# Gated linear attention and a gated FFN on one core: K and Q of rows 1 to 3 spread by DMA, outer products in the scan's layout, gate and state in PSUM

## The reference

```
q, k, v = x@Wq, x@Wk, x@Wv                      # 16 heads x 8
gate = exp(log_sigmoid(x@Wgk1@Wgk2 + b) / 16)   # per head and v channel
for t: S[h,v,k] = S[h,v,k]*gate[t,h,v] + v[t,h,v]*k[t,h,k]
       o[t,h,v] = sum_k S[h,v,k]*q[t,h,k]
x = layernorm(x + (layernorm(o)*gamma + beta) * silu(x@Wg) @ Wout)
```

```
h = silu(x@w1*s1) * (x@w2*s2)                   # 128 -> 512
h = gelu(h@h1*s3);  h = gelu(h@h2*s4)           # 512 -> 512, twice
x = layernorm(x + h@w3*s5)                      # 512 -> 128
```

## Time and profile before

| | us |
|---|---|
| median of three runs | 193.88 |
| the profiled execution | 193.71 |
| its span, first to last instruction | 191.9 |
| TensorE busy (matmuls) | 162.0 |
| VectorE busy | 147.9 |
| ScalarE busy | 117.5 |
| GpSimd busy | 113.8 |
| mean granted TensorE clock, share of full speed | 0.982 |
| DMA: 8.65 MB, mean 45 GB/s, nearly all ahead of 25 us | |

### The profile page before, as it was taken

One profiled execution on the slowest core, in us unless ns is written; L12 is line 12 of the kernel. 1 busy time (PEld: TensorE's weight loads), 2 busy tenths in 40 slices (PEclk: granted clock), 3 DMA queues, 4 the chain that ended last, 5 costly groups with the idle time before them and its releaser, 6 DMA issues.

```text
span 191.9 us, 2751 instructions
## 1 busy us (share of the span) xinstructions
PE 162.0 (84%) x790; PEld 124.0 (65%) x790; DVE 147.9 (77%) x301; ACT 117.5 (61%) x188; POOL 113.8 (59%) x94
## 2 busy tenths in 40 slices
PE   1859988969499997999999699999987999799840
PEld 1638656849387774878768487677856866567630
DVE  1398886988788997998999997899999685512360
ACT  4633649898037725378682556768454688979623
POOL 8989589919706689580677688427782313470011
PEclk9999999999979999999999999999999999999996
DMA  3999700000000000000000010000000100002002
GB/s 119 332 419 405 274 3 0 0 0 3 0 3 0 0 2 0 3 2 0 0 0 0 0 41 14 0 0 0 3 0 0 56 0 0 0 0 60 0 3 58
DMA packets 6191, 8.65 MB, mean 45 GB/s; under 512 B 513, under 2 KB 5026, under 8 KB 5666
## 3 DMA queue, kind: packets, MB, share of 16 engines
q1 hardware_dynamic: 5602, 5.60, 9.1%
q0 software_dynamic: 576, 2.88, 3.9%
HBM read 7.43 MB, written 1.05 MB: 44 GB/s over the span
## 4 chain that ended last, share of the span: by engine, by line
PE 25%; DVE 18%; issue 8%; ACT 5%; POOL 4%; DVEq 1%; POOLq 0%; ACTq 0%
PE ffn L600 8%; PE ffn L591 8%; DVE state L994 5%; DVE y L1005 2%; DVE y L1009 2%; DVE f_lo L1091 1%; ACT f_hi L831 1%; PE ffn L569 1%; DVE o_acc L1012 1%; DVE ffn L1080 1%; PE att L526 1%; POOL u_tok L313 1%; PE ffn L574 1%; ACT f_hi L839 1%; POOL o_rstd L332 1%
## 5 line engine op out<-in xcount | busy, mean ns | idle before, releaser
L354 POOL TENSOR_TENSOR f_lo<-full,f_hi 128x512 fp32r<-128x512 f32 x20 | 26.0, 1315 | 30.4 <-DVE full L1080 19.5
L994 DVE TENSOR_TENSOR_SCAN state<-gate,att 128x512 f32<-128x512 f32 x32 | 38.4, 1210 | 3.0 <-PE att L515 3.0
L839 ACT ACTIVATE f_hi<-ffn,vec_cols 128x512 fp32r<-128x512 f32 x32 | 22.1, 690 | 27.4 <-PE ffn L600 27.2
L591 PE MATMUL ffn<-f_hi,h_hi 128*128 128x512 f32 x128 | 36.7, 405 | 1.7 <-ACT f_hi L831 1.3
L600 PE MATMUL ffn<-f_lo,h_hi 128*128 128x512 f32 x128 | 35.6, 399 | 0.0
L591 PEld LDWEIGHTS ffn<-f_hi,h_hi 128*128 128x128 f32 x128 | 23.5, 188 | 8.7 <-ACT f_hi L831 3.0
L1091 DVE TENSOR_TENSOR f_lo<-ffn,f_hi 128x512 fp32r<-128x512 f32 x28 | 18.9, 687 | 12.4 <-ACT ffn L842 11.4
L600 PEld LDWEIGHTS ffn<-f_lo,h_hi 128*128 128x128 f32 x128 | 23.9, 188 | 5.8 <-DVE f_lo L1091 0.4
L313 POOL TENSOR_TENSOR u_tok<-kv_tok 128x1024 f32<-128x1024 f32 (+1 forms) x12 | 27.3, 2282 | 0.5 <-issue 0.4
L328 POOL TENSOR_TENSOR o_acc<-o_acc,y 128x512 f32<-128x512 f32 x16 | 20.6, 1290 | 7.9 <-DVE y L1005 7.8
L1005 DVE TENSOR_TENSOR y<-att,state 128x512 f32<-128x512 f32 x32 | 21.1, 671 | 0.0
(11 more groups left out here) (162 smaller groups left out, 318.6 us busy)
## 6 DMA issues: line engine op xcount, KB each, us to landing
h_raw<-in_hT SPq DMA_DIRECT2D x2, 1024.0 KB, 11.3
h_hi<-in_hT POOLq DMA_DIRECT2D x2, 1024.0 KB, 11.7
x_tok<-in_x SPq DMA_DIRECT2D x4, 256.0 KB, 5.0
out<-out_tok SPq DMA_DIRECT2D x3, 256.0 KB, 2.3
w_raw<-in_w12T SPq DMA_DIRECT2D x1, 512.0 KB, 4.6
w_hi<-in_w12T POOLq DMA_DIRECT2D x1, 512.0 KB, 8.1
xT_raw<-in_xT SPq DMA_DIRECT2D x1, 256.0 KB, 2.6
proj_raw<-in_proj SPq DMA_DIRECT2D x2, 128.0 KB, 2.3
```

What stands on the lines that cost most here:

```text
L354: nc.gpsimd.tensor_tensor(lo[:, o], full_block(layer, o), hi[:, o].bitcast(F32), ALU.subtract).then_inc(pool_rested, 1)
L591: nc.tensor.matmul(bank[:], h_hi[:, layer - 1, c, tile(o)], src_hi[:, c], start=(c == 0), stop=False)
L839: nc.scalar.activation(hidden[layer][0][:, o], bank[:], ACT.Gelu, scale=scales[:, 1 + layer, o:o + 1]).then_inc(gelu_hi_ready, 1)
L994: nc.vector.tensor_tensor_scan(state[:, k % 3], gate[:, b], A[2 + k % 2][:], 0.0, ALU.mult, ALU.add).then_inc(scanned, 1)
```

## The change

For rows 1 to 3, K, V and Q are projected with channels on the partitions. ScalarE copies them out (`keep_k`, `keep_v`, `keep_q`). K and Q of a row (256 KB each) are stored to device memory and read back by eight transfers of 512 KB (`spread`), each for two k, in which every partition (h, v) gets the row (h, k), so head rows are read eight times. GpSimd forms u for two k at a time from V and the spread K. The scan reads `GATE`, a PSUM bank into which ScalarE copies the row's gate, and u in SBUF; the state lies in two PSUM banks. Row 0 keeps outer products by token, transposes and replication. The last two sums over k become centring matmuls of y[2] and y[3]; the variance of o comes from a square on ScalarE and four one-column matmuls. The normalised x2 is written straight into `x_tok`. All loops are unrolled, and the order of every stream is new. In it, scans 0 and 1 and read-out 0 of the next row stand before the FFN's first layer.

```diff
-        A = [ctx.enter_context(nc.psum_tensor(f"att{i}", [P, L], F32)) for i in range(4)]
+        GATE = ctx.enter_context(nc.psum_tensor("gate_now", [P, L], F32))
+        S = [ctx.enter_context(nc.psum_tensor(f"state{i}", [P, L], F32)) for i in range(2)]
+        T = ctx.enter_context(nc.psum_tensor("att", [P, L], F32))
+        K_BANK = (None, F[2], F[1], F[1])
+        V_BANK = (None, F[3], F[2], F[2])
# SyncE
+            def spread(dst, rows, n, loaded):
+                heads = rows[:, 2 * n * L:2 * (n + 1) * L].unsqueeze(1).to_broadcast([HEADS, DH, 2 * L])
+                sp.dma_start(dst[:, 2 * n:2 * n + 2].rearrange("p k t -> p (k t)"), heads).then_inc(loaded, 16)
+            def load_k(b, n):
+                sp.wait_ge(k_stored[b - 1], 16)
+                if b == 1:
+                    sp.wait_ge(uT_ready, DH)
+                else:
+                    sp.wait_ge(u_ready, 4 * (b - 2) + n + 1)
+                spread(k_rep, k_rows[b - 1], n, k_rep_loaded[n])
...
+            store_k(1)
+            store_q(1)
+            load_k(1, 0)
+            load_k(1, 1)
+            load_q(1, 0)
+            load_k(1, 2)
+            load_k(1, 3)
+            load_q(1, 1)
+            load_q(1, 2)
+            load_q(1, 3)
# GpSimd
+            def outer_products(b, n):
+                pool.wait_ge(k_rep_loaded[n], 16 * b)
+                pool.wait_ge(v_kept, b)
...
+                slot = 2 * ((n + 1) % 2)
+                nc.gpsimd.tensor_tensor(u[:, slot:slot + 2], v_own[:, b - 1].unsqueeze(1).to_broadcast([P, 2, L]),
+                                        k_rep[:, 2 * n:2 * n + 2], ALU.mult).then_inc(u_ready, 1)
+            for a in range(1, B):
+                outer_products(a, 2)
+                rest(a - 1, 0, 0)
+                rest(a - 1, 0, 1)
+                rest(a - 1, 0, 2)
+                sum_over_k(a, (1,))
+                outer_products(a, 3)
+                rest(a - 1, 1, 0)
+                sum_over_k(a, (2,))
+                rest(a - 1, 1, 1)
+                sum_over_k(a, (3, 4, 5))
+                if a >= 2:
+                    e_rstd_of(a - 2)
+                if a + 1 < B:
+                    outer_products(a + 1, 0)
+                o_rstd_of(a)
+                r_rstd_of(a)
+                if a + 1 < B:
+                    outer_products(a + 1, 1)
# TensorE
+            def center_o(b):
+                if b >= 2:
+                    pe.wait_ge(e_sum_ready, b - 1)
+                pe.wait_ge(y_ready, DH * b + (8 if b == 0 else 7))
+                nc.tensor.matmul(T[:], center[:], y[:, 2], start=True, stop=False)
+                pe.wait_ge(y_ready, DH * b + 8)
+                nc.tensor.matmul(T[:], center[:], y[:, 3], start=False, stop=False)
+                pe.wait_ge(summed, (DH - 3) * (b + 1))
+                nc.tensor.matmul(T[:], center[:], o_acc[:], start=False, stop=True).then_inc(centered, 1)
+            def variance_o(b):
+                pe.wait_ge(sq_ready, b + 1)
+                for j in range(TILES):
+                    last = nc.tensor.matmul(S[1][:, j:j + 1], o_sq[:, tile(j)], ones[:], start=True, stop=True)
+                last.then_inc(o_var_sum_ready, 1)
+            def step(a, with_lo):
+                f = a - 1
+                for o in range(OB):
+                    ffn_hidden(f, 1, o, with_lo)
+                    ffn_hidden_rest(f, 1, o)
+                ffn_hidden(f, 2, 0, with_lo)
+                ffn_hidden_rest(f, 2, 0)
+                ffn_hidden(f, 2, 1, with_lo)
+                ffn_hidden_rest(f, 2, 1)
+                center_o(a)
+                ffn_hidden(f, 2, 2, with_lo)
+                variance_o(a)
+                project_out(a)
+                ffn_hidden_rest(f, 2, 2)
+                ffn_hidden(f, 2, 3, with_lo)
+                ffn_hidden_rest(f, 2, 3)
+                ffn_out_hi(f, with_lo)
+                ffn_out_rest(f)
+                transpose_x2(a)
+                first_layer(a, with_lo)
# TensorE, prologue from k = 5 of row 0
+            replicate_q0(5)
+            pe.wait_ge(x_lo_ready, 4)
+            project_k(1)
+            pe.wait_ge(z_log_ready, 2)
+            project_v(1)
+            pe.wait_ge(z_log_ready, 3)
+            project_q(1)
+            transpose_u0(6)
+            replicate_q0(6)
+            pe.wait_ge(z_log_ready, 4)
+            project_k(2)
+            pe.wait_ge(k_kept, 1)
+            project_v(2)
+            transpose_u0(7)
+            replicate_q0(7)
+            pe.wait_ge(v_kept, 1)
+            project_q(2)
+            pe.wait_ge(q_kept, 1)
+            project_g(0)
+            pe.wait_ge(k_kept, 2)
+            project_k(3)
+            project_beta(0)
+            center_o(0)
+            pe.wait_ge(v_kept, 2)
+            project_v(3)
+            pe.wait_ge(q_kept, 2)
+            project_q(3)
+            variance_o(0)
+            project_out(0)
# ScalarE
+            def step(a):
+                f = a - 1
+                ffn_gelu(f, 2, 0)
+                if a + 1 < B:
+                    place_gate(a + 1)
+                ffn_gelu(f, 2, 1)
+                square_o(a)
+                if a >= 2:
+                    out_normalise(a - 2)
+                ffn_gelu(f, 2, 2)
+                ffn_gelu(f, 2, 3)
+                nc.scalar.preload_act_table_set(SILU_SET)
+                round_x2(a)
+                scale_y(f)
+                first_layer(a)
# ScalarE, prologue, its end
+            keep_k(2)
+            keep_v(2)
+            keep_q(2)
             nc.scalar.preload_act_table_set(SILU_SET)
             silu_of_g(0)
             fold_beta()
+            keep_k(3)
+            sum_lo(1)
+            place_gate(1)
+            square_o(0)
+            keep_v(3)
+            keep_q(3)
             sum_lo(2)
             sum_lo(3)
-            round_q(3)
-            sum_lo(4)
             silu_of_g(1)
             silu_of_g(2)
-            sum_lo(5)
             silu_of_g(3)
+            sum_lo(4)
+            sum_lo(5)
             round_x2(0)
# VectorE
+            def scan(b, k):
+                if k % 2 == 0:
+                    dve.wait_ge(u_ready, 4 * (b - 1) + k // 2 + 1)
...
+                if k >= 2:
+                    dve.wait_ge(y_ready, DH * b + k - 1)
+                nc.vector.tensor_tensor_scan(s_bank(k)[:], GATE[:], u[:, (k + 2) % 4], 0.0, ALU.mult,
+                                             ALU.add).then_inc(scanned, 1)
+            def period(a):
+                f = a - 1
+                ffn_product(f, 0)
+                ffn_product(f, 1)
+                if f >= 1:
+                    add_x2(f - 1)
+                ffn_product(f, 2)
+                ffn_product(f, 3)
+                scan(a, 2)
+                read_out(a, 1)
+                rest(f, 0, 3)
+                scan(a, 3)
+                read_out(a, 2)
+                if f >= 1:
+                    e_statistics(f - 1)
+                scan(a, 4)
+                read_out(a, 3)
+                scan(a, 5)
+                rest(f, 1, 2)
+                read_out(a, 4)
+                if f >= 1:
+                    e_mean_and_variance(f - 1)
+                scan(a, 6)
+                rest(f, 1, 3)
+                read_out(a, 5)
+                scan(a, 7)
+                read_out(a, 6)
+                read_out(a, 7)
+                rest(f, 2, 0)
+                rest(f, 2, 1)
+                apply_gate(a)
+                o_variance(a)
+                if a + 1 < B:
+                    scan(a + 1, 0)
+                add_x(a)
+                rest(f, 2, 2)
+                rest(f, 2, 3)
+                x2_normalise(a)
+                if a + 1 < B:
+                    scan(a + 1, 1)
+                rest_of_x2(a)
+                if a + 1 < B:
+                    read_out(a + 1, 0)
```

More of the change, by code:

```diff
@@ L84, in gla_ffn_kernel @@
         gate = sb("gate", [P, B, L])
-        u_tok = sb("u_tok", [P, TILES, DH, P])
-        state = sb("state", [P, 3, L])
-        o_acc = sb("o_acc", [P, L])
-        o_stats = sb("o_stats", [P, TILES, 6])
-        o_mv = sb("o_mv", [P, TILES, 2])
+        u = sb("u", [P, 4, L])
+        o_sq = sb("o_sq", [P, L])
         o_var = sb("o_var", [P, TILES])
@@ new lines, in _ @@
+            store_q(1)
[7 more added lines that the diff above has]
+            load_q(1, 3)
+            store_k(2)
+            store_q(2)
+            store_k(3)
+            store_q(3)
+            for b in (2, 3):
+                load_k(b, 0)
+                load_k(b, 1)
+                load_q(b, 0)
+                load_k(b, 2)
+                load_q(b, 1)
+                load_k(b, 3)
+                load_q(b, 2)
+                load_q(b, 3)
+                if b == 3:
+                    store_out(0)
@@ L321, in sum_over_k @@
                     if k == 1:
-                        if not (isinstance(b, int) and b == 0):
-                            pool.wait_ge(oT_ready, b)
+                        if b >= 1:
```

(40 more changed lines are left out.)

684 lines of the change are left out of this document (292 added, 392 removed).

## The result

The changed kernel takes 206.75 us (median of 4 runs, 205.13 to 207.81); the kernel before takes 193.94 beside it. The ratio is 1.064, interval 1.059 to 1.070: **slower by 6.4%**, where 191.9 was forecast with a range of 187.5 to 197.5. Ratios leave out executions more than 1.5% above the fastest of the same kernel; medians and spreads hold all of them. Its profiled execution took 207.67, span 206.0.

What follows compares the result with a forecast made beforehand. VectorE's work ahead of R, the serial end of attention and the prologue were taken to bound it. 57.85 + 33.8 + 32.7 + 32.6 + 33.2 gave a 190.15 span, 1.8 less than before: 191.9 us, range 187.5 to 197.5.

Steps and rivals of the forecast that it cites:

- Ahead of R: Walk from S to R in the second period: VectorE sets the pace, removed TensorE work counts nothing; R at S + 20.8.
- rival a: Thinned TensorE falls to half clock at holes, 1.5 us each; one fall in each of four rows costs 6: 197.9; chance 0.14.
- R: End of a row's last attention read-out on VectorE; S + 18.27 before, forecast at S + 20.8.
- S0: First matmul of the first row's first FFN layer, ending the prologue; forecast 57.85 against 55.65, +2.2.
- S: First matmul of a row's first FFN layer; a period runs from it to the next row's.
- From R on: Serial attention end from R to the next row's S: shorter chain, 11.9 us forecast where 17.12 was taken before.
- the stall of 0.38: Stall at 172.50 in the last row, read as the loop's exit; claimed gone with unrolling, within that row's -1.3.
- rival (b): Prologue stays as long as before because its engines have holes: 189.3; chance 0.20.
- (c): 24 scans and 12 scan waits on VectorE dearer by 0.15 each, three quarters on the path: +4, 195.9; chance 0.14.
- (d): K or Q loads of row 1 land late, so transfers are not hidden: 196; chance 0.06.
- the 0.12: Wait of a scan for the read-out just issued, with two state banks instead of three tiles; 0.12, three or four times.

Runs made afterwards that it cites:

- run 7: Kernel before, with only TensorE's transposes of u and q-replicating matmuls thinned for rows 1 to 3 (wrong output there): 194.64 us, ratio 1.003.
- run 2: Changed kernel plus matmuls whose results are overwritten, eight ahead of hidden block (2,0) and three behind x2's transposes, in the steady periods: 201.9 us, ratio 1.037.
- run 5: run 2 plus the output row's variance-plus-epsilon and negated mean moved from VectorE to GpSimd: 200.45 us, ratio 1.035.
- run 12: Changed kernel plus only the three overwritten matmuls behind x2's transposes, none ahead of block (2,0): 203.91 us, ratio 1.048.
- run 10: run 9 without any overwritten matmul: 192.86 us, ratio 0.992 against the kernel before.
- run 11: run 9 with overwritten matmuls re-placed (seven during TensorE's wait, three ahead of the count) and three output second halves ahead of x2's transposes: 193.36 us, ratio 0.995.
- run 3: Changed kernel with remainder (1,3) ahead of scan 6, output mean and variance behind read-out 5, plus two and three overwritten matmuls: 203.91 us, ratio 1.051.
- run 4: Changed kernel with only the prologue reordered (row 0's last transposes and centring earlier, weight sums spread, flag behind normalisation): 204.72 us, ratio 1.056.
- run 6: run 2 without the 16 loads of K and Q for rows 2 and 3 (output wrong there): 201.7 us, ratio 1.037.
- run 9: run 8 with FFN banks turned by two, first halves laid into TensorE's wait, comparison ahead of GpSimd's product, twelve overwritten matmuls: median 192.82 us, ratio 0.981 (short executions).
- run 8: Changed kernel with the additions of run 2 and run 5, run 4's order modified, and scan 2, normalisation and x2 transposes earlier: 195.22 us, ratio 1.004.

## Why the prediction was wrong

**The step that failed** is the first edit of "Ahead of R": TensorE's 24 sets of transposes and 48 replicating matmuls "I count both as nothing", because VectorE sets R. That they gain nothing is right (run 7). But they were TensorE's work in its waits, and without them the clock falls: rival a, which had 0.14 at 6 us. The falls cost some 8 us of the 15.9 by which the span was missed (runs 2, 5 and 12). They also undo the premise itself: with the first layer at half clock R came 1.3 late, so VectorE alone did not set it. The counter-argument to rival a, "1.76 before 109.56 left the clock at 1.00", was read from a kernel in which that wait followed denser work. Run 7 took this work away; the wait became 2.09, and the clock fell behind it in one period of two. That the thinned work is the cause in the changed kernel, and not its other, longer waits, is argued from this run and from run 2, which put work back; no run parts the two fully.

The sum, part by part, in the span of the profiled execution (190.15 forecast, 206.0 measured):

| part | forecast | measured | clock | small operation | left |
|---|---|---|---|---|---|
| to S0 | 57.85 | 60.93 | 1.6 (run 5) | 1.8 (run 10) | -0.3 |
| period 1 | 33.8 | 34.24 | - | - | 0.4 |
| period 2 | 32.7 | 37.29 | 2.5 (run 2) | 0.9 (run 5) | 1.2 |
| period 3 | 32.6 | 37.29 | 2.5 | 0.9 | 1.3 |
| last row | 33.2 | 36.25 | 1.4 (run 2) | - | 1.7 |
| sum | 190.15 | 206.0 | 8.0 | 3.6 | 4.3 |

The second column of causes, the small operation, is a step that the prediction priced at 0.16 to 0.17 (it took the output row's mean and variance at 0.6, and the comparison by its row). Neither waited before, since GpSimd was between passes; the change moved both under passes of GpSimd. The clock's terms are differences between single profiled executions, and falls come and go in executions of the same code: the last row took 34.88 in run 2 without a fall and 36.7 in run 5 with one.

What is left, 4.3, are steps that were a little too short. R comes at S + 21.0 without fall and stall (20.8 said): this walk was right. From R on it is 12.9 (11.9 said): the output layer's last half waits for remainder (2,3), and x2's transposes stand behind it. Run 11, with the transposes ahead of that half, has 11.7. In the last row the fourth weight block begins at S + 7.5 (6.7 said), and the stall of 0.38, said to be gone with the loop, is there again at 186.18 and in each row of the unrolled code: it was not the loop's exit, as the prediction had read it. One sum in the prediction is off: with the prologue's 2.2 taken out, rival (b) stands at 189.7, not 189.3.

The Trainium skill ("TensorE: Matmul & The Clock Gate", "HAM oscillation") tells of short bursts of matmuls with waits between them, behind each of which the clock is low again; the prediction set one row against it. That it comes again row after row, the runs bear out, and at shorter waits than those of the page's example: behind 2.0 to 2.8 us, behind one of 0.81 (run 11), and in the first hidden layer behind waits of 0.5 to 1.1. But waits of 2.51 (run 3), 2.09 (run 7), 2.03 (run 12) and 2.02 (runs 5 and 12) were followed by full clock, the last one by half clock in other executions of the same code.

**Rivals.** (b), prologue no longer than before: wrong; but another order took 4.5 us off it, some 1.6 of them clock (run 4), so more than the 2.2 forecast for it could be had back. (c), dearer scans: 1.22 to 1.23 in PSUM, wrong. The wait of a scan for its read-out is 0.12 to 0.15 (a pair takes 1.83 where it took 1.70), as taken. (d), late loads: wrong (no scan waits for a load; and run 6 for rows 2 and 3).

Without clock and stalls the changed kernel's span would be near 194.4, its time near 196, still above the kernel before (191.9 and 193.9). So even with both terms known the change was no gain as ordered. Something of what was saved on VectorE came back only when TensorE's work was laid into its wait (runs 9 and 10, 0.6% by the medians of all executions).

**Left open:** which pattern of TensorE's work lets its clock fall. The executions of one kernel differ (run 8: clocks of 0.936 to 0.973, 3 us), so part of it is not set by the code, and no run tells what made run 9's longer executions long. A third state bank, which would take away the 0.12, was not tried: all eight banks are in use.

## What to carry to other kernels

Work on TensorE that costs nothing may be what keeps its clock up: before taking it out, ask what TensorE does in the waits that stay, and lay real work there (first halves of later blocks, by another use of the banks) in the same edit. Full clock behind a wait in the trace of before doesn't promise it in the kernel after. Compare two kernels' stages from the start of the stage, not by the time in the trace. Small VectorE operations from SBUF to SBUF are priced by what GpSimd is doing at that moment: put them where it waits, or on it.

## What the runs showed of the hardware

- VectorE's `tensor_scalar` of 4 or 6 fp32 elements a partition, SBUF to SBUF: 0.16 to 0.17 us alone; under a GpSimd `tensor_tensor` 1.01 to 1.98, ending within 0.04 of GpSimd's pass each time. A second one right behind it is fast (1.24, then 0.16). Passes of VectorE that read PSUM, and its statistics, ran at their usual time beside GpSimd's. The Trainium skill ("VectorE: DVE Perf Modes", "What auto-detection actually checks") lists a single source and the destination in SBUF, with outermost sizes even or equal, as what puts an operation into a mode of two ports. The small operations meet this; that the ports are why they stand is not tested here. An operation that doesn't meet it stood too: the sum of two SBUF tiles in the kernel before took 1.38 under a GpSimd pass, and the next one, without a pass, 0.69.
- At half clock 512-column matmuls follow each other every 0.427 us instead of 0.234, for 3 to 6 us a fall, and a fall on the path cost 1.2 to 1.9 us.
- Sixteen loads of 512 KB, at 114 GB/s in the second period (window of run 2), lengthened no period by a tenth of a us (34.80 without, 34.81 with).
